# Reordering the transfers that the SyncE queue issues in each step of an attention and FFN kernel

## The reference

```
x = x + xattn(layernorm(x), ctx)    # 8 heads of 32, 120 keys, softmax, out @ Wo + bo
h = layernorm(layernorm(x), g1, b1n)
h = bitlinear(h, w1, b1)            # rows rounded to 8 bits, weights to -1, 0, 1; 256 -> 1024
h = layernorm(gelu(h), g2, b2n)
x = x + bitlinear(h, w2, b2)        # 1024 -> 256
```

## Time and profile before

| | us |
|---|---|
| median of three runs | 1116.73 (1115.44 to 1118.75) |
| profiled execution, its own time | 1116.73 |
| its span in the trace | 1115.0 |
| DVE busy | 1028.7 |
| PE busy | 962.5 |
| ACT busy | 925.2 |
| POOL busy | 725.1 |

### The profile page before, as it was taken

How to read it: one execution, slowest core, us unless ns; L and a number is a source line. 1 busy time by engine, 2 the same in 40 slices (tenths; PEclk the granted TensorE clock), 3 DMA queues, 4 the chain that set the end, 5 groups by cost and what they waited for, 6 DMA issues and landing times.

```text
span 1115.0 us, 29852 instructions
## 1 busy us (share of the span) xinstructions
PE 962.5 (86%) x9614; PEld 646.5 (58%) x9649; DVE 1028.7 (92%) x1398; ACT 925.2 (83%) x2589; POOL 725.1 (65%) x1056
## 2 busy tenths in 40 slices
PE   4899999999999999999999757877777877777775
PEld 3677667666767777777776334444444444444443
DVE  1599989999989999999999899999999999999997
ACT  3688788788878888888886868999999999999993
POOL 4256556777666666666666575777777777777776
PEclk8999999999999999999999878999999999999998
DMA  5589986666687676676754312223333222333334
GB/s 142 129 152 184 178 151 170 157 157 153 139 165 165 146 162 164 156 159 159 160 139 103 84 34 28 32 36 38 38 38 38 36 31 36 38 38 38 38 36 70
DMA packets 145433, 114.74 MB, mean 103 GB/s; under 512 B 52536, under 2 KB 135864, under 8 KB 145360
## 3 DMA queue, kind: packets, MB, share of 16 engines
q1 hardware_dynamic: 127776, 96.90, 39.4%
q0 software_dynamic: 16864, 16.26, 12.4%
q10 hardware_dynamic: 720, 0.66, 0.2%
HBM read 71.75 MB, written 33.63 MB: 95 GB/s over the span
## 4 chain that ended last, share of the span: by engine, by line
DVE 34%; PE 31%; issue 25%; DMA 5%; POOL 2%; DVEq 1%; ACT 1%; SPq 1%; POOLq 0%; ACTq 0%
DVE gn_low L809 7%; DVE gn_high L809 7%; PE banks L1368 6%; PE banks L1359 6%; DVE nm_part L709 4%; DMA r_rows<-x_r 4%; PE banks L1283 4%; PE banks L1313 3%; PE banks L1322 2%; PE banks L1343 2%; DVE gn_low L795 2%; PE banks L1333 2%; DVE gn_high L795 2%; DVE h L755 1%; DMA r_bc<-r_rows 1%
## 5 line engine op out<-in xcount | busy, mean ns | idle before, releaser
L1014 ACT ACTIVATE probs<-banks 120x512 f32<-120x512 f32 x256 | 132.2, 603 | 51.2 <-PE banks L1299 51.2
L709 DVE TRANSPOSE_TENSOR_REDUCE nm_part<-banks 128x64 f16<-128x2048 f32 x64 | 147.7, 2308 | 3.5 <-PE banks L1283 3.2
L1054 ACT ACTIVATE g_dev<-g,g_sum 128x1024 bf16<-128x1024 f32 x128 | 149.0, 1164 | 0.0
L1059 ACT ACTIVATE g<-banks,h_dq 128x1024 f32<-128x1024 f32 x128 | 142.4, 1129 | 5.0 <-PE banks L1216 3.9
L1368 PE MATMUL banks<-wo_sb,o_t 128*128 128x256 f32 x512 | 136.4, 399 | 0.0
L1246 PE MATMUL banks<-w_t,g_t 128*128 128x256 bf16 x1008 | 122.1, 275 | 14.4 <-ACT g_t L1092 11.7
L518 POOL COPY h_dq<-h_cl 128x2 f32<-128x2 f32 (+1 forms) x64 | 13.7, 214 | 184.9 <-DVE h_qs L767 183.8
L1210 PE MATMUL banks<-w_t,h_t 128*128 128x512 bf16 x471 | 120.1, 393 | 5.7 <-ACT g L1059 3.6
L1246 PEld LDWEIGHTS banks<-w_t,g_t 128*128 128x128 f16 x1008 | 94.4, 98 | 52.6 <-issue 27.6
L1359 PE MATMUL banks<-xt,wq_c 128*128 128x256 f32 x512 | 121.3, 380 | 0.0
L592 POOL TENSOR_TENSOR g_r<-g_ve,neg_half 128x2 f32<-128x2 f32 x64 | 105.2, 1644 | 5.8 <-ACT g_ve L1075 5.8
(11 more groups left out here) (177 smaller groups left out, 2733.7 us busy)
## 6 DMA issues: line engine op xcount, KB each, us to landing
x_in<-in_x SPq DMA_DIRECT2D x64, 256.0 KB
xt<-in_x_t SPq DMA_DIRECT2D x64, 256.0 KB, 4.6
xr<-in_x SPq DMA_DIRECT2D x64, 256.0 KB, 4.4
out<-xr SPq DMA_DIRECT2D x64, 256.0 KB, 6.4
out<-res POOLq DMA_DIRECT2D x62, 256.0 KB, 4.3
ctx_t<-in_ctx_t SPq DMA_DIRECT2D x64, 128.0 KB
r_bc<-r_rows SPq DMA_DIRECT2D x64, 128.0 KB, 4.2
w_raw<-in_w_t SPq DMA_DIRECT2D x8, 256.0 KB, 7.9
```

The source lines that it names most:

```text
L709: dve.tensor_reduce(nm_part[:, :, 0:C * RB], blocks_p, AX.X, ALU.max, negate=True, apply_transpose=True).then_inc(max_done, 1)
L1014: act.activation(probs[:, p, j, :, :], sc_p[0:KV, j, :, :], ACT.Exp, scale=SCALE).then_inc(probs_done, 1)
L1054: act.activation(g_dev[:, t, :], g[:, p, t, :], ACT.Square, scale=-float(F), bias=g_sum[:, p, t:t + 1], accum_out=g_ssq[:, p, t:t + 1]).th ...
L1059: act.activation(g[:, p, t, :], u_p[t], ACT.Gelu, scale=h_dq[:, b, t:t + 1], accum_out=g_sum[:, p, t:t + 1]).then_inc(gelu_done, 1)
```

## The change

In the SP queue's attn the blocks of a step are put in another order. Before: turn, x_in, ctx_t and xt, r_bc, xr, out, store of x_r. After: turn, out, r_bc, ctx_t and xt, x_in, store of x_r, xr. The last block is also moved by one batch: step i loads xr of batch i and not of batch i - 1, and so waits for the landing of the out that was issued in the same step. Nothing else is changed.

```diff
                     b = i - 5
                     if live(b, NB):
                         turn_rows(b, (n + 3) % 4)
-                    b = i + 5
-                    if live(b, NB):
-                        after(sp, x_ssq, (b - 1) * T)
-                        sp.dma_start(x_in[:, q, :, :], x[b]...).then_inc(x_loaded[q], 16)
+                    b, r = i - 4, n
+                    if live(b, NB):
+                        sp.wait_ge(b2_done, b + 1)
+                        sp.dma_start(out[b]..., xr[:, r, :, :]).then_inc(x1_stored[r], 16)
+                    b = i + 2
+                    if live(b, NB):
+                        after(sp, q_done, b - 1)
+                        sp.wait_ge(r_stored[p], (b - p) * 8 + 16)
+                        sp.dma_start(r_bc[:, p, :], r_rows[b]...).then_inc(r_loaded[p], 16)
                     b = i + 3
                     if live(b, NB):
                         after(sp, q_done, b - 1)
                         sp.dma_start(ctx_t[:, q, :, :], ctx_t_in[b]).then_inc(ctx_loaded[q], 16)
                         after(sp, h_centred, b - 6)
                         sp.dma_start(xt[:, q, :, :], x_t[b]).then_inc(xt_loaded[q], 16)
-                    b = i + 2
-                    if live(b, NB):
-                        after(sp, q_done, b - 1)
-                        sp.wait_ge(r_stored[p], (b - p) * 8 + 16)
-                        sp.dma_start(r_bc[:, p, :], r_rows[b]...).then_inc(r_loaded[p], 16)
-                    b, r = i - 1, (n + 3) % 4
-                    if live(b, NB):
-                        after(sp, x1_stored[r], (b - r) * 4)
-                        sp.dma_start(xr[:, r, :, :], x[b]...).then_inc(xr_loaded[r], 16)
-                    b, r = i - 4, n
-                    if live(b, NB):
-                        sp.wait_ge(b2_done, b + 1)
-                        sp.dma_start(out[b]..., xr[:, r, :, :]).then_inc(x1_stored[r], 16)
+                    b = i + 5
+                    if live(b, NB):
+                        after(sp, x_ssq, (b - 1) * T)
+                        sp.dma_start(x_in[:, q, :, :], x[b]...).then_inc(x_loaded[q], 16)
                     b = i + 3
                     if isinstance(i, int) and i == -3:
                         store_r(0, 0)
                         store_r(1, 1)
                     elif live(b, NB) and not (isinstance(i, int) and i == -2):
                         store_r(b, q)
+                    b, r = i, n % 4
+                    if live(b, NB):
+                        after(sp, x1_stored[r], (b - r) * 4)
+                        sp.dma_start(xr[:, r, :, :], x[b]...).then_inc(xr_loaded[r], 16)
```

More of the change, by code:

```diff
@@ L395, in attn @@
                         turn_rows(b, (n + 3) % 4)
-                    b = i + 5
+                    b, r = i - 4, n
                     if live(b, NB):
-                        after(sp, x_ssq, (b - 1) * T)
-                        sp.dma_start(x_in[:, q, :, :], x[b].rearrange("(t p) n -> p t n", p=P)).then_inc(x_loaded[q], 16)
+                        sp.wait_ge(b2_done, b + 1)
+                        sp.dma_start(out[b].rearrange("(t p) n -> p t n", p=P), xr[:, r, :, :]).then_inc(x1_stored[r], 16)
+                    b = i + 2
+                    if live(b, NB):
+                        after(sp, q_done, b - 1)
+                        sp.wait_ge(r_stored[p], (b - p) * 8 + 16)
+                        sp.dma_start(r_bc[:, p, :], r_rows[b].rearrange("(a n) -> a n", a=1).to_broadcast([P, ROWS])).then_inc(r_loaded[p], 16)
                     b = i + 3
@@ L405, in attn @@
                         sp.dma_start(xt[:, q, :, :], x_t[b]).then_inc(xt_loaded[q], 16)
-                    b = i + 2
+                    b = i + 5
                     if live(b, NB):
-                        after(sp, q_done, b - 1)
-                        sp.wait_ge(r_stored[p], (b - p) * 8 + 16)
-                        sp.dma_start(r_bc[:, p, :], r_rows[b].rearrange("(a n) -> a n", a=1).to_broadcast([P, ROWS])).then_inc(r_loaded[p], 16)
-                    b, r = i - 1, (n + 3) % 4
-                    if live(b, NB):
-                        after(sp, x1_stored[r], (b - r) * 4)
-                        sp.dma_start(xr[:, r, :, :], x[b].rearrange("(t p) n -> p t n", p=P)).then_inc(xr_loaded[r], 16)
-                    b, r = i - 4, n
-                    if live(b, NB):
-                        sp.wait_ge(b2_done, b + 1)
-                        sp.dma_start(out[b].rearrange("(t p) n -> p t n", p=P), xr[:, r, :, :]).then_inc(x1_stored[r], 16)
+                        after(sp, x_ssq, (b - 1) * T)
+                        sp.dma_start(x_in[:, q, :, :], x[b].rearrange("(t p) n -> p t n", p=P)).then_inc(x_loaded[q], 16)
                     b = i + 3
@@ L424, in attn @@
                         store_r(b, q)
+                    b, r = i, n % 4
+                    if live(b, NB):
+                        after(sp, x1_stored[r], (b - r) * 4)
+                        sp.dma_start(xr[:, r, :, :], x[b].rearrange("(t p) n -> p t n", p=P)).then_inc(xr_loaded[r], 16)
                 steps(sp, A0, NB + 5, L0, L1, attn, 4, aside)
```

## The result

The reordered kernel is slower: 1122.09 us median (1120.07 to 1126.05, 8 runs) beside 1118.3 us (1115.44 to 1121.39, 8 runs) for the kernel before on the same chip, a ratio of 1.0052, 95% interval 1.0032 to 1.0073. The two medians alone give 1.0034; the record has 25 executions of the reordered kernel in all, with a median of 1124.18 us, and their mean is 1.0052 times that of the eight of before. The forecast was 1113.6 us in a range up to 1120.7, so the median lies above the range and on the other side of "no change". The profiled execution took 1124.81 us, 8.1 us more than the one of before.

A forecast was written before the change was run, and what follows sets the result against it. The prediction took DVE (92% busy) and TensorE as having no room, leaving only DVE's waits for r_bc. Start -1.6, later waits -2.0 and weight laps +0.5 summed to -3.1 us: 1113.6 us, range 1110.8 to 1120.7.

The forecast's parts named there:

- One lap of the steady loop: Attention stage's SP queue: r_bc issued 0.25 us later with 1.7 us to spare; moving x_in, ctx_t and xt later costs nothing.
- the new wait: SP waits for the landing of out issued in the same step; hidden except in weight-load laps, +0.5 us (0 to 4).
- The start: First r_bc load, with 640 KB less in front, takes 3.7 us instead of 5.27: -1.6 us (-2.4 to nothing).
- The five later waits: DVE's other waits for r_bc, 3.5 us, put down to late stores of x_r: -2.0 us (-3.5 to nothing).
- SP is held by its own store: Rival, steady loop: out keeps landing above 7.0 us and lengthens SP's lap; +8 us, 1125 us, chance 0.13.
- r_bc is held by the store in front of it: Rival, steady loop: r_bc cannot report before out, taking 6.2 us where 5.9 are free; 1132 us, chance 0.11.
- Nothing moves: Rival: the x_r store lands late by itself and the first r_bc stays slow; time stays 1116.7 us, chance 0.21.
- if ACT is seen waiting for x_in: Sign in the new profile that would show the prediction wrong; x_in's later issue had been costed at nothing.

The follow-up runs named there:

- o_start_new: Kernel before, with the new order only in the steps ahead of step 0 and the old order from step 0 on; 1116.99 us, ratio 0.9982 to the kernel before.
- n_wide_store: Reordered kernel with the 1 KB store written as 16 pieces of 64 B of a constant instead of the row scales; 1113.05 us, ratio 0.9973 to the kernel before.
- o_xr_late: Kernel before with only xr changed: batch i, loaded at the end of the step; 1188.33 us, ratio 1.0625 to the kernel before.
- n_pool_store: Reordered kernel with the store of the row scales issued by GpSimd on its own queue; 1131.55 us, ratio 1.0146 to the kernel before.
- o_xin_late: Kernel before with only x_in moved, to behind out and ahead of the store of x_r; 1131.90 us, ratio 1.0110 to the kernel before.
- n_xr_mid: Reordered kernel with xr of batch i - 1 put between x_in and the store of x_r; 1124.81 us, ratio 1.0085 to the kernel before.
- n_xr_guard: Reordered kernel with xr of batch i put between x_in and the store of x_r; 1126.10 us, ratio 1.0096 to the kernel before.
- o_wide_store: Kernel before with the 1 KB store written as 16 pieces of 64 B of a constant; 1113.92 us, ratio 0.9987 to the kernel before.

## Why the prediction was wrong

**The step that failed** is the sentence on x_in in *One lap of the steady loop*: "x_in moves by 5.2 us; ACT begins on one at 475.65 and on this one a lap and more later, near 484.8, so 7.3 us are left where the longest landing of a 128 KB r_bc was 6.5: nothing". The 7.3 us were right: the lap at 509.89 had 7.6. The landing was wrong. It was borrowed from a transfer of half the size in another place, and in its new place x_in took 5.0 us in the median and up to 9.9. The rows of out were the ones to read, not those of r_bc: out stood directly ahead of the store of x_r and took 6.8 us, up to 9.7, for the same 256 KB. x_in took over out's place, and with it the tail of its landing (9.9 us beside 9.7), though not the median (5.0 beside 6.8). The experiments put this down to the 128 small pieces of the store. I named out's neighbours as the cause when I costed the new wait and the rivals, and did not carry the same cause to x_in. Priced so, the step would have read: 9.7 us at worst where 7.3 are free, up to 2.4 us on ScalarE in some laps. Measured: 9.1 us on ScalarE in 8 laps, 6.1 us of it reaching DVE.

**The start, -1.6 us.** The mechanism was right and its size nearly so: DVE's first wait for r_bc fell from 10.6 to 9.4 us, by 1.2. But it did not last to the end of the start. One step ran at a lower granted clock, and nm_part of that step started 0.76 us late instead of 0.81 us early. That the clock would answer to the earlier start, I had not considered. o_start_new, with the start alone, is 2.0 us faster in the timed runs (0.4 to 3.6).

**The five later waits, -2.0 us.** They fell from 3.5 to 3.1 us: 0.4. SP's waits for the store of x_r at the line of r_bc went from 49.5 to 28.0 us, so lateness did go, though SP may only have waited that time out at the line of out ahead of it (174.9 us for POOL). The store still took 6.2 us in the median; the trace of before has no landing of it. I had put its lateness down to the 512 KB around it; n_wide_store shows that its own 128 pieces make about half of it (median landing 3.1 us with 16 of them, line 385).

**The new wait, +0.5 us.** SP waited 4.5 us in 5 laps, 1.8 us at most, and none of it is seen on DVE; out lands in 3.3 us where I expected 5 to 6 and the limit was 7.0. So no loss is seen here, and this term was right within its ends.

**The sum.** Forecast -1.6 - 2.0 + 0.5 = -3.1. The profiled execution: start +0.8 (by 46 us), inv_part behind x_in +6.1, r_bc -0.4, one wait of DVE for TensorE's scores +1.4, 7.9 in all, where nm_part of the last step is 7.4 us late; the second stage adds 0.7 us. The timed ratio puts the whole at 1.0052 x 1118.3 - 1118.3 = 5.8 us (3.6 to 8.2).

**The rivals.** *SP is held by its own store* gave 1125 us, near the measured time, for a reason that did not occur: its condition, out above 7.0 us, was never met (5.6 at most). A wait of that kind came in o_xr_late, where SP stood 239.6 us for out. Its price was also built on little: the profile has the landing of one out in four before, 14 of the 59 behind the earlier trace rows and 3 of the 11 behind the earlier trace rows (7.8, 8.0 and 4.7 us), so "7.8 us in 11 laps" was the median of three. *r_bc is held by the store in front of it* did not occur either: r_bc took 4.4 us in the median and 6.4 at most, over the 5.9 us limit only at its tail. Its condition was met in so far as r_bc never landed ahead of the out issued before it, in 58 laps of 58, but it came 2.6 us behind it in the median, so out did not set when it landed. *Nothing moves* was right about the late store and missed what the store does to its neighbour. The last line of the prediction did name the sign to look for, "if ACT is seen waiting for x_in", without giving it a price or a chance.

**What stays open.** Why x_in lands together with the store behind it in some laps and well ahead of it in the others; how much of what x_in gains from the wide store comes from its neighbour and how much from 16 DMA engines that are less busy throughout; what part of n_pool_store's loss is GpSimd's; and how a store of real row scales in few pieces would do, since both wide versions store a constant. Of the kernels that compute everything, the fastest is o_start_new, 0.9982 of the kernel before.

## What to carry to other kernels

A landing time belongs at least as much to a place in the queue as to a transfer: when a load is moved, price it with the landing of what stands in the new place now, tail included, and not with that of a similar load elsewhere. Look for the transfer of very small pieces first: moving the loads around it only chose who pays (x_in, r_bc, xr or SP), while fewer pieces took all the waits of DVE and ScalarE for transfers away in either order. With the 128 pieces kept, none of the other orders of the steady loop that were tried beat the old one, in which out, with a lap to spare, stands beside the store.

## What the runs showed of the hardware

- A store of 1 KB took 6.2 us in the median in 128 pieces of 8 B and 3.1 us in 16 of 64 B (reordered kernel, 60 to 610 us); in 256 pieces of 4 B it made the kernel 18% slower. In the old order with 16 pieces it landed in 1.4 us.
- On SP's queue no transfer landed ahead of the one issued just before it, in 460 pairs of neighbours of the reordered kernel (60 to 610 us); the smallest distance was 0.16 us.
- A 256 KB store to HBM landed in 3.3 us away from that small store (reordered kernel) and in 6.8 us directly ahead of it (before, 14 landings), and the weight loads (256 KB) in 7.1 us beside the 128 pieces and 4.3 us beside 16.
- The granted clock of TensorE fell to 0.57 to 0.63 in 40 to 44 us in the reordered kernel, o_start_new, n_wide_store, o_xin_late and n_xr_mid, all five with an earlier start. It stayed at 1.00 there before, and in n_pool_store, n_xr_guard and o_wide_store, which also start earlier (o_wide_store had 0.74 in 32 to 36 us instead). TensorE had been busy 4.00 us of 32 to 36 and 2.4 to 3.0 us of 36 to 40 in all of these, so its busy time alone does not tell them apart.
